# A recommendation tower in fp32: layer 0 of the cross network in six full tiles and one pass over 40 leftover pairs

## The reference

```
e = stack([tbl_f[ids[:, f]] for f in range(39)], axis=1)      # 2048 x 39 x 16
x0 = xk = e
for W, b in ((w0, b0), (w1, b1), (w2, b2)):                   # 39 x (39 or 64) x 128
    z = relu(einsum('bhd,bkd,hks->bsd', x0, xk, W) + b)       # all pairs (h, k), per d
    xk = z[:, :64]; direct.append(z[:, 64:])                  # last layer: all of z is direct
logit = sum(concatenate(direct, axis=1), axis=-1)             # sum over d
h = relu(concat([logit, dense_ctx]) @ W_top1 + b_top1)
y = relu(h @ W_top2 + b_top2) @ W_top3
```

## Time and profile before

| what | value |
|---|---|
| median of 3 runs | 2544.88 us (2543.24 to 2546.89) |
| the profiled execution | 2545.02 us, span in the trace 2543.1 us |
| PE, DVE, ACT, POOL busy | 96%, 89%, 46%, 61% of the span |
| granted TensorE clock | 0.995 of full speed |
| moved by DMA | 477 MB, 188 GB/s in the mean |
| HBM read | 469 MB |

### The profile page before, as it was taken

The page is one execution under the profiler, slowest core; times in us unless marked ns, Lnnn a source line. Parts: engine busy times, 40 slices in busy tenths (PEclk is TensorE's granted clock), DMA queues, the critical chain, the costliest instruction groups (busy, mean ns, idle before and its releaser), DMA issues.

```text
span 2543.1 us, 25999 instructions
## 1 busy us (share of the span) xinstructions
PE 2432.8 (96%) x7712; PEld 1423.5 (56%) x7712; DVE 2268.7 (89%) x1356; ACT 1175.5 (46%) x1414; POOL 1557.9 (61%) x1029
## 2 busy tenths in 40 slices
PE   0599999999999999999999999999999999999999
PEld 0265555556555555555555565555556555555553
DVE  0599999999999999999999999999999999999960
ACT  0244444445454444545444444444444444445442
POOL 6476667667666766766676666667666766743240
PEclk9899999999999999999999999999999999999999
DMA  2986777777677777867777776787777677766610
GB/s 69 246 211 180 199 207 202 180 217 214 176 198 205 207 178 215 209 182 197 209 206 177 217 206 190 190 211 210 178 207 205 200 184 213 207 182 194 195 30 0
DMA packets 262712, 477.02 MB, mean 188 GB/s; under 512 B 19500, under 2 KB 37788, under 8 KB 262614
## 3 DMA queue, kind: packets, MB, share of 16 engines
q1 hardware_dynamic: 141766, 271.07, 38.9%
q10 hardware_dynamic: 100480, 200.29, 28.5%
q0 software_dynamic: 20448, 5.45, 1.4%
HBM read 468.99 MB, written 7.74 MB: 187 GB/s over the span
## 4 chain that ended last, share of the span: by engine, by line
PE 73%; POOL 10%; DVE 6%; issue 4%; DMA 4%; ACT 2%; SPq 0%; POOLq 0%; DVEq 0%; ACTq 0%
PE z L693 37%; PE z L716 33%; POOL emb L352 5%; DVE prod L418 4%; POOL pair_lo L211 4%; DMA emb<-in_tbl,idx 3%; PE xk L775 1%; PE z L775 1%; DMA x_pairs<-x_transposed 1%; ACT pair_hi L532 1%; POOL half_parts L207 1%; DVE pair_lo L211 1%; PE turned L674 1%; DVE logit L448 1%; ACT xk L542 0%
## 5 line engine op out<-in xcount | busy, mean ns | idle before, releaser
L418 DVE TENSOR_TENSOR prod<-x_pairs,xk 128x2048 f32<-128x2048 f32 x640 | 1436.4, 2284 | 75.2 <-PE z L716 46.9
L693 PE MATMUL z<-prod,w_plain 128*128 128x512 f32 (+2 forms) x2944 | 1383.1, 594 | 40.5 <-DVE prod L418 40.5
L532 ACT CAST pair_hi<-prod 128x1024 fp32r<-128x1024 f32 x703 | 735.4, 1046 | 1085.2 <-PE z L716 793.6
L211 POOL TENSOR_TENSOR pair_lo<-prod,pair_hi 128x1024 fp32r<-128x1024 f32 x320 | 764.1, 2388 | 638.3 <-ACT pair_hi L532 621.7
L693 PEld LDWEIGHTS z<-prod,w_plain 128*128 128x128 f32 (+2 forms) x2944 | 555.4, 189 | 474.1 <-issue 394.9
L352 POOL DMA_INDIRECT emb<-in_tbl,idx x624 | 701.3, 1124 | 184.0 <-issue 173.7
L716 PE MATMUL z<-pair_hi,w_lo 128*128 128x512 f32 (+1 forms) x1408 | 786.6, 559 | 2.3 <-DVE pair_lo L211 1.7
L716 PE MATMUL z<-pair_hi,w_hi 128*128 128x512 f32 (+1 forms) x1408 | 555.7, 395 | 0.0
L716 PE MATMUL z<-pair_lo,w_hi 128*128 128x512 f32 (+1 forms) x1408 | 555.1, 394 | 0.0
L211 DVE TENSOR_TENSOR pair_lo<-prod,pair_hi 128x1024 fp32r<-128x1024 f32 (+1 forms) x384 | 468.5, 1220 | 48.7 <-ACT pair_hi L532 48.7
L716 PEld LDWEIGHTS z<-pair_hi,w_lo 128*128 128x128 f32 (+1 forms) x1408 | 265.2, 188 | 297.2 <-POOL pair_lo L211 135.8
(11 more groups left out here) (50 smaller groups left out, 566.5 us busy)
## 6 DMA issues: line engine op xcount, KB each, us to landing
x_pairs<-x_transposed SPq DMA_DIRECT2D x64, 2432.0 KB, 16.9
x_pairs<-x_transposed ACTq DMA_DIRECT2D x64, 2432.0 KB, 19.3
x_diag<-x_transposed SPq DMA_DIRECT2D x128, 546.0 KB
x_diag<-x_transposed ACTq DMA_DIRECT2D x64, 546.0 KB
x_pairs<-x_transposed SPq DMA_DIRECT2D x64, 256.0 KB, 20.4
emb<-in_tbl,idx POOLq DMA_INDIRECT x624, 6.3
x_diag<-x_transposed SPq DMA_DIRECT2D x128, 78.0 KB
x_transposed<-stage SPq DMA_DIRECT2D x32, 156.0 KB
```

The source lines that it names most:

```text
L211: engine.tensor_tensor(pair_lo[0:rows, pair % PAIR_RING], held[0:rows, at:at + 2, :], pair_hi[0:rows, pair % PAIR_RING].bitcast(F32), ALU. ...
L418: nc.vector.tensor_tensor(prod[0:rows, pos % RING, 0:n, :], a, xk.unsqueeze(1).broadcast_to([rows, n, N]), ALU.mult).then_inc(prod_ready, 1)
L532: nc.scalar.copy(pair_hi[0:rows, pair % PAIR_RING], held[:, at:at + 2, :]).then_inc(hi_ready, 1)
L693: ins = nc.tensor.matmul(z[n][:], w, held[0:rows, i, :], start=(k == 0 and i == plain[0]), stop=(k == last_slot and not here and i == plai ...
```

## The change

Layer 0 is laid out anew, without the seventh tile and its 78 pairs. The six tiles that stay get 11 more rows each (`EXTRA`, 128 rows in all); in four of the tiles these rows have weights, so they take over 44 of the 78 pairs. The other 34 are loaded with zero-weight rows between them as four runs of ten rows (`small_rows`), three times over: 40 rows as low parts, 40 and 40 as high parts, 120 partitions in all. One single-pass instruction contracts them with weights laid out to match. GpSimd makes the product (`small_product`) and later the low part (`small_low`), ScalarE the high part and a masking (`small_hi`).

Splits: layer 0 splits four of its six tiles, so twelve pairs are split in a chunk (with layers 1 and 2 unchanged in what they split). The engine of each low part is written in `SPLITS`: all of layer 2's and one pair of layer 1's on GpSimd, the rest on VectorE. For layer 1's low parts on VectorE, ScalarE makes a second copy of the high part in PSUM (`hi_copy`, the two banks that the transposes also use), which VectorE reads; `direct01` lies in PSUM too and holds the half tile's copy. High and low parts have a ring of six tiles instead of four. TensorE handles layer 2's split tiles one slot behind the plain ones (`BEHIND`), and layer 0 as one piece that frees both of its slots at the end. The copy `xk0` shares its bank with `xk2`.

Order: the transposes of a group come behind layer 0 in chunk 1, `fill_stage` behind layer 0's hand-over, the gathers between layer 1's low part and the small low part on GpSimd, in other portions (20 to 29 in chunk 0, then 30 to 38, 0 to 9 and 10 to 19). The sums of the direct outputs go to small windows and are stored to DRAM by SyncE once a group and table (`store_window`), and loaded again for the tower. In the prologue 34 loads, some very small, build the weights of layer 0.

The core of the diff:

```diff
-R0_LAST = 2 * F
+TF = T0 - 1
+EXTRA = P - R0
+FEW, RUNS, TERMS = 10, 4, 3
+SMALL = FEW * RUNS
+SMALL_ROWS = TERMS * SMALL
 TX = 20
 WRAP = 20
 COLS = B * D
 QUAD = 4
 RING = 4
-SL0, SLX = -(-T0 // QUAD), TX // QUAD
+SL0, SLX = -(-TF // QUAD), TX // QUAD
 SLC = SL0 + 2 * SLX
-L0_FIRST = range(0, T0, QUAD)
+L0_FIRST = range(0, TF, QUAD)
...
-SPLITS = {0: [(0, 0, 2)],
-          1: [(0, 0, 2), (1, 0, 2), (2, 0, 2), (2, 3, 1), (3, 0, 2), (4, 0, 2)],
-          2: [(0, 0, 2), (1, 0, 2), (2, 0, 2), (2, 3, 1), (3, 0, 2), (4, 0, 2)]}
-EARLY = {1: 4, 2: 4}
+V, G = "VectorE", "GpSimd"
+SPLITS = {0: [(0, 0, 2, V), (0, 2, 2, V)],
+          1: [(0, 0, 2, V), (1, 0, 2, V), (2, 0, 2, G), (2, 3, 1, V), (3, 0, 2, V), (4, 0, 2, V)],
+          2: [(0, 0, 2, G), (1, 0, 2, G), (2, 0, 2, G), (2, 3, 1, G), (3, 0, 2, G), (4, 0, 2, G)]}
+EARLY = {1: 5, 2: 4}
+def splits_in(n, k):
+    return [s for s in SPLITS[n] if s[0] == k]
+BEHIND = {1: False, 2: True}
...
-GATHERS_AHEAD = 30
-GATHERS_AT = [range(30, F), range(0, 10), range(10, 20), range(20, 30)]
-PAIR_RING = 2
-PAIRS = {n: sum(m == 2 for _, _, m in SPLITS[n]) for n in SPLITS}
-assert CHUNKS * sum(PAIRS.values()) % PAIR_RING == 0
+def lows(n, engine):
+    return sum(who == engine for _, _, _, who in SPLITS[n])
+LOWS_C = {who: sum(lows(n, who) for n in SPLITS) for who in (V, G)}
+COPIES_C = lows(1, V) + lows(2, V)
+assert lows(0, G) == 0
+GATHERS_AHEAD = 20
+GATHERS_AT = [range(20, 30), range(30, F), range(0, 10), range(10, 20)]
+PARTS = 6
...
+        def extra_rows(engine, chunk):
+            shifted = bass.AP(tensor=chunk.tensor, offset=chunk[DIAG * TF:].offset,
+                              ap=[[COLS, EXTRA], [COLS, TF], [1, N]])
+            engine.dma_start(x0_diag[R0:P, 0:TF, :], shifted).then_inc(x0_diag_in, 16)
+            engine.dma_start(x0_diag[R0:P, TF, :], chunk[0:EXTRA]).then_inc(x0_diag_in, 16)
+        def small_rows(engine, chunk):
+            for dst, first, step in ((small_base, EXTRA, 0),
+                                     (small_prod, EXTRA + DIAG * TF, COLS)):
+                src = bass.AP(tensor=chunk.tensor, offset=chunk[first:].offset,
+                              ap=[[step, RUNS], [COLS, FEW], [1, N]])
+                for term in range(TERMS):
+                    engine.dma_start(dst[term * SMALL:(term + 1) * SMALL], src).then_inc(small_in, 16)
...
                 chunk = xt[:, bass.ds(first, N)]
                 for i in range(DIAG - 1):
                     diag_band(sp, chunk, i)
+                extra_rows(sp, chunk)
+                if not (isinstance(bt, int) and bt == c == 0):
+                    sp.wait_ge(small_lo_ready, sums)
+                small_rows(sp, chunk)
...
+                    if c == 0:
+                        sp.wait_ge(summed01, bt * CHUNKS + 1)
+                        store_window(0, bt)
+                    if c == 1:
+                        sp.wait_ge(summed2, bt * CHUNKS + 2)
+                        store_window(1, bt)
                     if c == 2 and not last:
                         store_group(bt + 1)
                     if c < CHUNKS - 1:
...
+            def small_product(n):
+                pool.wait_ge(small_in, 16 * SMALL_DMAS * (n + 1))
+                nc.gpsimd.tensor_tensor(small_prod, small_prod, small_base[:], ALU.mult
+                                        ).then_inc(small_ready, 1)
+            def small_low(n):
+                pool.wait_ge(small_masked, n + 1)
+                nc.gpsimd.tensor_tensor(small_parts[:], small_prod, small_parts[:].bitcast(F32),
+                                        ALU.subtract).then_inc(small_lo_ready, 1)
...
-                pair = PAIRS[0]
-                fields_done = 0 if isinstance(bt, int) and bt == GROUPS - 1 else GATHERS_AHEAD
                 for c in range(CHUNKS):
                     chunk = bt * CHUNKS + c
-                    pool.wait_ge(gathered, 16 * ((bt + 1) * F + fields_done))
-                    fields = fields_at[c]
-                    if fields and fields[0] == 0:
+                    split, pos = len(SPLITS[0]) + chunk * SPLITS_C, SL0 + c * SLC
+                    end = isinstance(bt, int) and bt == GROUPS - 1 and c == CHUNKS - 1
+                    if not end:
+                        small_product(chunk + 1)
+                    done = lows_of(1, chunk, 0, split, pos)
+                    if c == 2 and len(fields_at[c]):
+                        start_group(bt + 2, False)
+                    gather(fields_at[c])
+                    if not end:
+                        small_low(chunk + 1)
+                    split, pos = split + len(SPLITS[1]), pos + SLX
+                    if not (isinstance(bt, int) and bt == GROUPS - 1 and c == CHUNKS - 1):
+                        split, pos = split + len(SPLITS[0]), pos + SL0
+                    lows_of(2, chunk, done, split, pos)
+                    if c == 1 and len(fields_at[2]):
+                        pool.wait_ge(gathered, 16 * (bt + 2) * F)
                         pool.sem_inc(waits_held, 1)
                         load_indices(bt + 2)
...
+            def products(n, copies, xk, slot, pos, late, split, chunk):
+                first_tile, rows, tiles = (FIRST_TILE, P, TX) if n else (L0_FIRST, P, TF)
+                for k, first in enumerate(first_tile):
+                    product(slot + k, pos + k, copies[0:rows, first:min(first + QUAD, tiles), :],
+                            xk[0:rows])
+                    split = subtract(late, split)
+                    late = splits_of(n, pos, k, chunk)
+                return late, split
...
+                    if n and who == V:
+                        copies = [s for s in SPLITS[n][0:i] if s[3] == V]
+                        if m == 1:
+                            nc.scalar.copy(direct01[0:HALF].bitcast(F32R), held[0:HALF, at, :]
+                                           ).then_inc(hi_copied, 1)
+                        else:
+                            if any(s[2] == m for s in copies):
+                                last = max(j for j, s in enumerate(copies) if s[2] == m)
+                                act.wait_ge(lo_ready[V],
+                                            len(SPLITS[0]) + chunk * LOWS_C[V] + last + 1)
+                            nc.scalar.copy(hi_copy[:, 0:m, :].bitcast(F32R), held[:, at:at + m, :]
+                                           ).then_inc(hi_copied, 1)
...
+            def small_hi(n):
+                act.wait_ge(small_ready, n + 1)
+                nc.scalar.copy(small_parts[:], small_prod).then_inc(small_hi_ready, 1)
+                act.wait_ge(small_hi_ready, n + 1)
+                nc.scalar.activation(small_prod, small_prod, ACT.Copy, scale=is_low[0:SMALL_ROWS]
+                                     ).then_inc(small_masked, 1)
...
-                    pair = round_splits(SPLITS[1][:EARLY[1]], P, slot, pos, pair, held_by)
+                    round_splits(1, slice(0, EARLY[1]), slot, pos, used_by, chunk)
                     direct_2(chunk, slot)
                     if not (last and c == CHUNKS - 1):
                         copy_xk0(chunk + 1)
-                    pair = round_splits(SPLITS[1][EARLY[1]:], P, slot, pos, pair, held_by)
+                    round_splits(1, slice(EARLY[1], None), slot, pos, used_by, chunk)
                     slot, pos = slot + SLX, pos + SLX
                     if not (last and c == CHUNKS - 1):
-                        pair = round_splits(SPLITS[0], R0, slot, pos, pair, held_by)
+                        round_splits(0, slice(0, None), slot, pos, used_by, chunk)
+                        small_hi(chunk + 1)
+                        act.wait_ge(prod_ready, slot + SL0)
                     hand_on(1, xk2, b1_sb, slot)
...
-                    if c == 1 and not last:
-                        fill_stage(bt + 1)
                     if last and c == CHUNKS - 1:
-                        round_splits(SPLITS[2], P, slot, pos, pair, held_by)
+                        round_splits(2, slice(0, None), slot, pos, used_by, chunk)
                     else:
                         slot, pos = slot + SL0, pos + SL0
-                        pair = round_splits(SPLITS[2][:EARLY[2]], P, slot, pos, pair, held_by)
+                        round_splits(2, slice(0, EARLY[2]), slot, pos, used_by, chunk)
                         hand_on(0, xk1, b0_sb, slot)
-                        act.wait_ge(summed01, chunk + 1)
+                        act.wait_ge(summed01, chunk + 2)
                         direct_0()
-                        pair = round_splits(SPLITS[2][EARLY[2]:], P, slot, pos, pair, held_by)
+                        if c == 1 and not last:
+                            fill_stage(bt + 1)
+                            act.wait_ge(stage_ready, 2 * (bt + 2))
+                        round_splits(2, slice(EARLY[2], None), slot, pos, used_by, chunk)
...
+                    if not BEHIND[n]:
+                        split_parts(n, k, lows)
+                    elif k > 0:
```

(27 more changed lines are left out.)

394 lines of the change are left out of this document (240 added, 154 removed).

## The result

The changed kernel takes 2999.32 us (median of 4 runs, 2976.32 to 3007.56), the kernel before 2544.27 beside it: ratio 1.177, 95% interval 1.171 to 1.184. The forecast was 2620, range 2470 to 2672: slower was right, by 76 us where 455 were measured. The place that the forecast named is where most of the time goes, but TensorE waits there some 23 us where 9.1 were forecast, and other places were not seen.

A forecast was written before the change was run, and what follows sets the result against it. TensorE bounds the kernel at 36.09 us a chunk, VectorE 1.3 us behind. Groups rise from 148.02 to 153.1 us (+76), other chunks -3.7, start +3: 2545 + 75.5 = 2620 us, range 2470 to 2672.

The forecast's parts named there:

- The place that the forecast named: Layer 1 of each group's third chunk: TensorE waits 9.1 us for GpSimd's pair behind the late small product.
- the step that decides: Moved transposes, stage filling and small product make SyncE's stores delay the small rows: 10.7 us lost once a group.
- ordinary chunks: Chunks without transposes or the late wait, walked through at a period of 35.45 us.
- Rival (a): Small rows come in time: every chunk takes 35.45 us, the group 142.7, time 2464 us; chance 0.28.
- D: Time from the start of SyncE's late loads until the small rows are in: between 10.2 and 17.6 us.
- D is 10.2 to 12.1 alone: SyncE's late loads without ScalarE's pairs: bands 8.4 us, extra and small rows 1.8 to 3.7 on top.
- I take 15: The value in us chosen for D, from two halves of the pairs landing side by side.
- Rival (b): Only four of 16 DMA engines carry the small loads: D grows by 3.5 us, time 2673 us; chance 0.18.
- up to 5.5 us of it is in the way: ScalarE's half of the next pairs, issued just ahead of SyncE's late loads, adds up to 5.5 us to D.
- a D near 17: The value of D if DMA engines take turns between queues; first come first served gives near 11.
- The start was put at +3 us: Kernel start: eight more loads ahead of the first pairs cost 3 us.
- Rival (c): No late rows, but the small low part behind ten gathers comes 1.5 us late every chunk: 2538 us; chance 0.07.

The follow-up runs named there:

- run 1: Changed kernel with SyncE's four stage stores issued behind the loads of the group's fourth chunk: 2718.79 us (one run).
- version 6: 4 with gathers dealt out: two ahead of layer 1's low part (not in the third chunk), six behind, small low part, then the rest: 2486.95 us.
- run 7: version 6 with layer 2's split tiles in their own slot, as in the kernel before: 2531.12 us.
- run 10: Changed kernel, but from the second chunk on each small load brings 64 of its 512 columns: 2820.63 us (one run).
- run 2: Changed kernel with the small rows reordered so each load's slowest dimension is ten, not four, weights laid to match: 2776.97 us (one run).
- run 13: Changed kernel with the window store of each group's first chunk behind the second chunk's loads: 2930.23 us (one run).
- 4: Changed kernel with stage stores and the first chunk's window store behind the loads, and small rows with slowest dimension ten: 2629.19 us.
- run 5: 4 with GpSimd's small low part behind the seventh gather of a chunk, not the last: 2625.81 us.
- 8: version 6 without ScalarE's second high copies in PSUM, so VectorE reads the high parts from SBUF: 2564.35 us.
- 12: version 6 with the small rows as in the change, slowest dimension four: 2516.17 us.

## Why the prediction was wrong in size

**What held.** The direction, and the step that decides: stage, stores and bands came within 0.3 us of the forecast, and run 1 shows the late wait to hang on that order. Layer 0 takes 4.76 us in version 6 (from 1240.46 to 1245.22), for 4.75, and ordinary chunks are 35.4 to 35.6 there, for 35.45 walked through. In the changed kernel itself they are 36.1 at best, and chunks above 36 were one of the forecast's own signs of being wrong. Rival (a), 2464 with a group of 142.7, is what version 6 nearly reaches, 2487 and 143.8. Putting layer 2 a slot behind is worth 44 us (run 7). Subtractions that read PSUM take 1.212 us, those from SBUF 1.217, as assumed; the small product takes 1.28, for 1.3 to 1.4.

```profile
L269 DVE TENSOR_TENSOR lo_parts<-prod,hi_copy 128x1024 fp32r<-128x1024 f32 x256 | 310.1, 1212 | 9.7 <-ACT hi_copy L727 9.7
...
L269 DVE TENSOR_TENSOR lo_parts<-prod,hi_parts 128x1024 fp32r<-128x1024 f32 x128 | 153.2, 1217 | 66.3 <-ACT hi_parts L713 66.3
```

**The term that failed: "D is 10.2 to 12.1 alone", "I take 15".** It measured 31.7. By the forecast's own sum a D of 31.7 gives a wait of 25.8 in layer 1 (TensorE's longest is 23.7) and 2620 + 15 x 16.7 = 2870. (The prediction's 2659 belongs to its upper bound of 17.6; a D of 17 gives 2650.) D has three parts:

- The small loads were costed by their bytes, at the pace of the pairs or of the bands, which comes to 1.4 to 2.8 us for their 480 KB. By run 10 seven eighths of these bytes are worth 7.6 to 8.4 us in the shape of the change, and by run 2 the same bytes in a better shape take 6.5 to 9.4 us less. Rival (b) had named this with 3.5 us and a chance of 0.18; it is true and was too cheap. Its price was a quarter of the full rate, with nothing beside it. By the rule of the Trainium skill, "DMA: Bandwidth & Descriptors", section "Why a DMA increments its semaphore by 16 and not by 1", four engines carry each of these loads and ten each of the spread ones; D's fall from 31.7 to 22.3 agrees, though no view here counts the engines of one load.
- What runs beside them: "up to 5.5 us of it is in the way". The same loads take 20.4 in the short case and 31.7 late, 11.3 more; with an eighth of the bytes 12.1 more. The forecast held ScalarE's pairs alone for this; the stores just ahead differ between the two cases too, and no run separates them. The rule in the Trainium skill, "DMA: Bandwidth & Descriptors", section "Queues, rings and completion order", that a DMA engine takes turns between queues, was worked out in the prediction to a D near 17; the direction agrees, the size doesn't.
- Twelve us in run 10's short case are the bands, the extra rows and the issue of 12 loads, with an eighth of the small rows' bytes. The forecast's 10.2 to 12.1 had all of these bytes in it, so this part was a little too small as well.

How the first two add up was not measured. That the small rows wait on their few engines behind a share of ScalarE's pairs would fit, and is only argued.

**Terms put at nothing or nearly so.** SyncE's two new window stores were listed as a part of the change but not costed, though the first waits for a sum that is ready only late in the chunk: ScalarE's band goes at 1335.29, SyncE's at 1342.12. In the view of what SyncE's queue waits for, in the changed kernel, the stage's stores and that window store (L392, for the sum of L623) lead:

```profile
SPq L352 <- ACT stage L696: 524.6, 16, 37.6
SPq L392 <- DVE logit L623: 378.0, 15, 25.4
```

By run 13 the second is worth 61 to 69 us, from single runs of a kernel whose four runs spread over 31 us; 4.8 us a group, 72 in all, is what its trace shows.

The start was put at +3 us. GpSimd's first wait for small rows is there, and by its first half-tile low part the start is 16.7 us later, in the kernel before and in the changed one:

```profile
132.62 1.30 POOL L207 TENSOR_TENSOR half_parts<-prod,half_parts 64x512 fp32r<-64x512 f32 x1
...
122.13 1.26 POOL L470 TENSOR_TENSOR x_diag<-x_diag,small_base 120x512 f32<-120x512 f32 x1 [34.89 <-DMA x_diag<-x_transposed]
...
149.31 1.28 POOL L263 TENSOR_TENSOR half_parts<-prod,half_parts 64x512 fp32r<-64x512 f32 x1
```

**Rival (c), and the wait for gathered rows.** Rival (c), the small low part behind ten gathers, had 1.2 us a chunk, 73 us, and a chance of 0.07. From 4 to 6 dealing the gathers gives 142 us. TensorE's wait for gathered rows, which the forecast didn't charge, falls by 68.8 us of it, to nothing. What is left is 73 us, the price of (c), and the two ordinary chunks fall by 1.2 us each (36.8 to 35.6). As far as that goes (c) was priced well and held to be too unlikely: it was true together with the late rows. The division is a subtraction, not a run of its own; run 5, which moves the small low part alone, gains 0.9 and 0.6 in two chunks and loses it again on the gathered rows.

**The sum again.** 2870, 72 for the window store and 14 for the start make 2956. The remaining 43, some 3 us a group, lie mostly in the chunks with no late wait: 36.1 where 35.45 was forecast in two of them, and 37.1 in the third once run 13 has taken the short wait away. The half clock behind each late wait, 3.6 us for 1.9, is 1.7 us within the late case, which came out 17.2 above the forecast where D alone gives 16.7.

## What to carry to other kernels

Ask of each store in an in-order DMA queue what it waits for and which loads stand behind it: here stores that gain nothing by their place held loads that an engine needed, and two moved blocks were worth 280 and some 70 us. Cost a small DMA by the dimension that spreads it and by what runs beside it, not by its bytes; 480 KB with a slowest dimension of four took 6.5 to 9.4 us more than with one of ten. A wait that feeds a critical loop must be measured with its sources removed one after the other: dealing out the gathers gave 142 us once the small rows came in time, and before that it lengthened one late path by as much as it shortened the rest.

## What the runs showed that was not expected

- The issue of a DMA can itself be held: 15.84 us for one load of pairs behind the late small rows, 0.69 for the same load in the next chunk. In versions 4 to 8, where no small rows are late, none takes over 3 us once the start is past. That the queue was full fits, and no view shows it.
- A gather started while VectorE makes two SBUF subtractions back to back lasts until after both are done, 3.51 us instead of 0.94. Beside a subtraction with one operand in PSUM it takes 0.94, and VectorE's subtraction 1.21.
- After the late wait TensorE's first eight instructions, 3.6 us, ran at a granted clock of 0.50 (1.2 GHz).
- One wait at the start can outweigh those of all groups: 15.5 of the 29 us between versions 12 and 6 lie ahead of the first chunk's end.
